# Turning x of the feed-forward: transposes of TensorE, or a DRAM write, a block read and 32x32 transposes of VectorE

## The chip, the cores and the metric

The kernel runs on one core of one Trainium2 chip. The metric is the time of one execution on the device in microseconds, as the median of several runs. The engines are TensorE (PE, its weight loads PEld), VectorE (DVE), ScalarE (ACT), GpSimd (POOL) and SyncE (SP), which only issues DMA transfers here.

## The reference

One block of a transformer with adaptive layer norm: linear attention, then a gated feed-forward, over 8192 tokens of 512 features.

```python
x = L0_attn_x                                  # (1, 8192, 512) float32
mod = (_silu(L0_c) @ L0_wmod).reshape(L0_c.shape[0], 6, 1, -1)
sa, ca, ga, sb, cb, gb = (mod[:, 0], mod[:, 1], mod[:, 2], mod[:, 3], mod[:, 4], mod[:, 5])
...
h = _layernorm(x, axis=-1) * (1 + ca) + sa
x = x + ga * _L0_attn_ref(h, ...)              # causal linear attention, 16 heads of 32
h = _layernorm(x, axis=-1) * (1 + cb) + sb
x = x + gb * _L0_ffn_ref(h, L0_ffn_w_gate, L0_ffn_w_up, L0_ffn_w_down)
...
# _L0_ffn_ref, weights int32, wg = w_gate / 127 and so on
gate = jnp.einsum('bsd,hd->bsh', x, wg)        # 512 -> 1536
up = jnp.einsum('bsd,hd->bsh', x, wu)
h = jax.nn.silu(gate) * up
return jnp.einsum('bsh,dh->bsd', h, wd)        # 1536 -> 512
```

## The kernel before

The kernel has two stages. The attention runs over 16 groups of 512 tokens up to some 1000 us; the feed-forward over 8 groups G of 1024 tokens (FT = 8 tiles of 128) fills the rest. Nothing is scheduled by a planner: each engine has its list of instructions, written out by hand, and waits on semaphores. An engine never goes past a wait that is not met.

**The steps of the feed-forward.** For its gate and up products a group needs x normalized and turned (features on the partitions). The 1536 hidden features are 12 blocks q. The 2x2 product of each block is done with seven products, p1 to p7 (L1859, four matmuls of 128x512 each, since both operands of x are split in a high and a low part), that go into four PSUM banks: xs (two), sums (two). In a step q (tensor `step`) TensorE issues p1(q), p7(q-1), p2(q), p5(q), p4(q-1), p6(q), p3(q). ScalarE copies p1, p5 and p6 out (save_p1, save_p5, save_u2), VectorE adds them up (add_c11 L1695, add_c12 L1701, add_c22 L1706) and multiplies with the gate (times_gate2 L1720, times_gate1 L1712), ScalarE and GpSimd split the product h in h_hi (L1586) and h_lo (h_low, L1488). In VectorE's step q the order is add_c22(q-1), add_c11(q), times_gate2(q-1), times_gate1(q-1), an aside, add_c12(q). Each product waits for the sum that frees its bank: p4(q) for add_c22(q), p5(q+1) for add_c12(q), p6(q) for add_c11(q).

**The halves.** After six blocks TensorE does the down products of that half (`down`, L1916, 8 row tiles into the banks dn[0..3]). p7(5) and p4(5) stand between the first ones: down 0, p7(5), down 1, p4(5), and so on. VectorE gates each result (gate_y, L1727) and GpSimd adds the residual (L1493), which SP has loaded (load_residual, L1402) and stores again. Before the last down the first three products of the next half or group are issued.

**The x of the next group.** SP loads it (load_x) into eight tiles xg: four of the attention's xg, two each of z_exp and z_relu. In the asides VectorE takes the statistics (norm_stats L1672, steps 2 to 5; norm_var in step 5), GpSimd makes rstd (rstd_of, L1483, behind h_low of q = 5), VectorE normalizes a pair of tiles at a time (norm_x, L1688, after add_c12(6) and in steps 7 to 9). TensorE turns: eight turns of four transposes (`turn`, L1927), 0 to 3 after steps 8 to 11 into dn, 4 to 7 between the downs into sums and xs. ScalarE evacuates each with scale and bias (evacuate, L1553) and makes the high parts (high, L1538). VectorE makes the four differences T1 to T4 (sum_of, L1662) and the low parts (low, L1666), in one long list behind step 11, with the gates of the second half between. The x of group 0 is turned by TensorE in the attention (x_turn L1088, turn_second L1096).

**The ring.** SP loads the weight parts of block q + 4 (load_parts, L1384, 1 MB) when p4(q) has freed their slot; stores, residuals, x and parts all stand in SP's one list.

## Time and profile before

| | |
|---|---|
| median of 3 runs | 2004.0 us (2003.52 to 2006.8) |
| the profiled execution | 2003.83 us, span 2002.1 us |
| TensorE busy | 1959.0 us, 98% |
| VectorE busy | 1455.2 us, 73% |
| ScalarE, GpSimd busy | 905.7 us, 869.1 us |
| moved by DMA | 309.81 MB |

The profile is one execution. Each engine's busy time is the sum of its instructions; a TensorE that is busy may still hold products that wait inside its pipeline, so stops are looked for in the timeline. The trace gives the start and duration of each instruction, and for an idle stretch before it the instruction that ended it.

### The profile page before, as it was taken

The numbers are of one execution on the slowest core, as the hardware profiler recorded it, in microseconds if no ns is written. First come the engines' busy times: TensorE is split into PE (matmuls) and PEld (weight loads), VectorE is DVE, ScalarE is ACT, GpSimd is POOL, SyncE is SP. The second block draws the span as 40 slices with busy tenths as digits, with TensorE's granted clock in tenths as the row PEclk, the third lists the DMA queues.
The fourth block names the chain that finished last, engine by engine and source line by source line (L and its number), as shares of the span: only waits on it lengthen the run. The fifth ranks groups of instructions, "written<-read, shape, count | busy, mean of one in ns | idle before, by whom it ended". The sixth has DMA issues, their size and how long they took to land. (4 is left out here: it accounts for less than half of the span.)

```text
span 2002.1 us, 43921 instructions
## 1 busy us (share of the span) xinstructions
PE 1959.0 (98%) x16008; PEld 1591.0 (79%) x16008; DVE 1455.2 (73%) x2409; ACT 905.7 (45%) x1542; POOL 869.1 (43%) x718
## 2 busy tenths in 40 slices
PE   7999999999999999999899999999999999999999
PEld 4788888888888888887678888888888888888887
DVE  7977888888888888887875857658576585765744
ACT  5443444344444344444254536445364453644533
POOL 2533544444544444443334444444434444344444
PEclk9999999999999999999999999999999999999999
DMA  7223333444433434433475654756546565465553
GB/s 268 70 90 104 117 118 119 130 134 127 127 112 121 135 121 136 129 101 99 152 284 178 209 172 148 228 168 210 174 147 224 168 210 182 143 219 170 170 170 106
DMA packets 202521, 309.81 MB, mean 155 GB/s; under 512 B 16145, under 2 KB 72977, under 8 KB 202386
## 3 DMA queue, kind: packets, MB, share of 16 engines
q1 hardware_dynamic: 201858, 306.78, 48.1%
q8 instruction: 107, 1.75, 0.4%
q10 hardware_dynamic: 528, 1.05, 0.1%
q14 instruction: 28, 0.23, 0.0%
HBM read 225.19 MB, written 82.58 MB: 154 GB/s over the span
## 5 line engine op out<-in xcount | busy, mean ns | idle before, releaser
L1488 POOL TENSOR_TENSOR h_lo<-y_rows,h_hi 128x512 fp32r<-128x512 f32 x192 | 246.5, 1303 | 368.1 <-ACT h_hi L1586 368.0
L460 POOL TENSOR_TENSOR x_res<-y,x_res 128x512 f32<-128x512 f32 x64 | 82.8, 1293 | 297.7 <-DVE y L871 287.8
L850 DVE TENSOR_TENSOR probs<-sc,causal 128x512 f32<-128x512 f32 x256 | 158.4, 679 | 5.4 <-PE sc L1147 5.2
L611 ACT ACTIVATE z_exp<-pj,qk_neg 128x512 f32<-128x512 f32 x128 | 87.9, 687 | 160.7 <-PE pj L1128 150.5
L1128 PE MATMUL pj<-xt_hi,w_hi 128*128 128x512 f32 x512 | 145.3, 405 | 12.0 <-DVE a_t L860 11.6
L1916 PE MATMUL sc<-wd,h_hi 128*128 128x512 f32 x384 | 150.6, 392 | 0.0
L1916 PE MATMUL sc<-wd,h_lo 128*128 128x512 f32 x384 | 149.7, 390 | 0.0
L449 POOL TENSOR_TENSOR a_lo<-a_t,a_hi 128x512 fp32r<-128x512 f32 x60 | 77.8, 1296 | 158.7 <-ACT a_hi L625 158.7
L1128 PE MATMUL pj<-xt_lo,w_hi 128*128 128x512 f32 x512 | 137.7, 390 | 1.7 <-DVE xt_lo L788 1.7
L1701 DVE TENSOR_TENSOR r_den<-pj,k_tok 128x512 f32<-128x512 f32 x96 | 66.2, 690 | 98.9 <-ACT k_tok L1569 54.6
L1128 PE MATMUL pj<-xt_hi,w_lo 128*128 128x512 f32 x512 | 137.3, 390 | 0.0
L1586 ACT ACTIVATE h_hi<-y_rows 128x512 fp32r<-128x512 f32 x192 | 119.0, 620 | 24.9 <-DVE y_rows L1720 13.4
L1564 ACT ACTIVATE k_tok<-sc 128x512 f32<-128x512 f32 x96 | 56.3, 586 | 158.7 <-PE sc L1859 158.7
L1128 PEld LDWEIGHTS pj<-xt_hi,w_hi 128*128 128x128 f32 x512 | 91.3, 188 | 39.2 <-DVE a_t L860 18.0
L596 ACT ACTIVATE xf<-sc,mod_col 128x512 f32<-128x512 f32 x64 | 49.9, 779 | 157.1 <-PE sc L1088 157.1
L444 POOL TENSOR_TENSOR prod<-k_sum,qt 128x512 f32<-128x512 f32 x64 | 94.4, 1475 | 61.1 <-DVE qt L796 42.2
L1128 PEld LDWEIGHTS pj<-xt_lo,w_hi 128*128 128x128 f32 x512 | 96.1, 188 | 23.1 <-DVE xt_lo L788 2.1
L1559 ACT ACTIVATE kv_diag<-pj 128x512 f32<-128x512 f32 x96 | 57.4, 598 | 123.3 <-PE pj L1859 122.5
L1128 PEld LDWEIGHTS pj<-xt_hi,w_lo 128*128 128x128 f32 x512 | 96.1, 188 | 20.5
L1574 ACT ACTIVATE k_sum<-r_den 128x512 f32<-128x512 f32 x96 | 60.7, 632 | 107.0 <-DVE y_rows L1712 94.4
L1712 DVE TENSOR_TENSOR y_rows<-sc,k_sum 128x512 f32<-128x512 f32 x96 | 66.3, 690 | 55.8 <-PE sc L1859 55.8
L1706 DVE TENSOR_TENSOR bv_row<-sc,kv_diag 128x512 f32<-128x512 f32 x96 | 66.3, 690 | 54.5 <-PE sc L1859 54.4
(247 smaller groups left out, 5403.5 us busy)
## 6 DMA issues: line engine op xcount, KB each, us to landing
w_hi<-parts SPq DMA_DIRECT2D x48, 1024.0 KB, 5.4
w_lo<-parts SPq DMA_DIRECT2D x48, 1024.0 KB, 5.3
x_mid<-x_res SPq DMA_DIRECT2D x96, 256.0 KB, 2.9
x_res<-in_L_attn_x SPq DMA_DIRECT2D x64, 256.0 KB, 2.8
k_dram<-k_block SPq DMA_DIRECT2D x252, 64.0 KB
xg<-in_L_attn_x SPq DMA_DIRECT2D x15, 1024.0 KB, 7.4
x_res<-x_mid SPq DMA_DIRECT2D x60, 256.0 KB, 4.0
full<-x_mid SPq DMA_DIRECT2D x60, 256.0 KB, 3.7
```

The costliest lines, as they stand in the source:

```text
L444: pool.tensor_tensor(out=prod[:, c % 2, :], in0=k_sum[:, c % 2, :], in1=qt[parity][:, c, :], op=ALU.mult).then_inc(prod_ready, 1)
L449: pool.tensor_tensor(out=a_lo[:, :], in0=a_t[:, :], in1=a_hi[:, :].bitcast(F32), op=ALU.subtract).then_inc(a_lo_ready, 1)
L460: pool.tensor_tensor(out=x_res[:, slot, :], in0=y[:, :], in1=x_res[:, slot, :], op=ALU.add).then_inc(y_ready, 1)
L611: act.activation(z_exp[:, n % 2, :], pj[:, n % 2, :], ACT.Relu, bias=qk_neg[:, 1 - kind, c:c + 1], scale=-scale).then_inc(below_ready, 1)
L850: dve.tensor_tensor(out=probs[:, h, :].rearrange("p (c i) -> p c i", c=C), in0=sc[:, h, :].rearrange("p (c i) -> p c i", c=C), in1=causal[ ...
L1128: mm = pe.matmul(to, w[:, k, at:at + P], xt[:, k, :], start=(i == 0), stop=(i == len(passes) - 1))
L1488: pool.tensor_tensor(out=h_lo[b], in0=h[i], in1=h_hi[b].bitcast(F32), op=ALU.subtract).then_inc(h_lo_ready, 1)
L1586: act.activation(h_hi[q % 6 * 2 + i], h[i], ACT.Copy).then_inc(h_hi_ready, 1)
L1701: dve.tensor_tensor(out=c12, in0=sums[1], in1=s12, op=ALU.add).then_inc(c12_ready, 1)
L1706: dve.tensor_tensor(out=c22, in0=xs[q % 2], in1=s5, op=ALU.add).then_inc(c22_ready, 1)
L1712: dve.tensor_tensor(out=h[0], in0=xs[q % 2], in1=gate[0], op=ALU.mult).then_inc(h1_ready, 1)
L1916: mm = pe.matmul(dn[i % 4], as_(part[j * 2 + t // GT][:, rows]), as_(wd[half * 6 + j]), start=(j == 0 and part is h_hi), stop=(j == 5 and ...
```

## The change

TensorE no longer turns x for groups 1 to 7. VectorE normalizes x as before; then SP writes each half of four tiles to a DRAM buffer xn_dram (save_xn, 1 MB) and reads it back in blocks (load_blocks: four transfers of 256 KB in runs of 512 bytes, each onto 32 partitions), so that 32 partitions hold the 32 tokens of a block for one quarter of the features. A 32x32 transpose of VectorE per bank (`turn`, 128x512, reading every fourth word) then writes the turned x to the same PSUM banks. The feature order that results is every fourth feature; the rows of the gate and up weights and of two modulation matrices are regrouped to it in their layout in DRAM, and TensorE's transposes for group 0 read every fourth word too. z_exp and z_relu become one buffer z.

The asides change: statistics in steps 1 to 4, norm_var in step 4, two pairs of norm_x in step 5 and two after add_c12(6) (group 0 keeps its statistics and norm_var, with two pairs after add_c12(6) and two in step 7). GpSimd makes rstd behind h_low of q = 4 (group 0: of q = 5). Turns 0 to 2 are asides of steps 9 to 11, turns 3 to 7 stand in the list behind step 11.

```diff
+        def regrouped(t, c):
+
+            return xg[:, t, :].rearrange("p (f c) -> p c f", c=C)[:, c, :]
+
         def x_turn(g, c, bank):
             wait(pe, xn_ready, g + 1)
             wait(pe, xf_ready, g * C + c - (C if isinstance(g, int) and g < 2 else 0))
             for t in range(GT):
-                mm = pe.transpose(bank[:, t * P:(t + 1) * P], xg[:, t, c * P:(c + 1) * P], ident[:, :])
+                mm = pe.transpose(bank[:, t * P:(t + 1) * P], regrouped(t, c) if isinstance(g, int) and g == NG
+                                  else xg[:, t, c * P:(c + 1) * P], ident[:, :])
             mm.then_inc(xt_ps, 1)
...
             for t in range(GT):
-                mm = pe.transpose(bank[:, t * P:(t + 1) * P], xg[:, t, c * P:(c + 1) * P], ident[:, :])
+                mm = pe.transpose(bank[:, t * P:(t + 1) * P], regrouped(t, c), ident[:, :])
             mm.then_inc(xt_ps, 1)
...
+        def save_xn(G, second):
+
+            wait(sp, xn_ready, G * 4 + (2 * second - 2))
+            sp.dma_start(xn_dram[second * GN:(second + 1) * GN, :].rearrange("(t p) d -> p t d", p=P),
+                         xg_halves[second][:, :, :]).then_inc(xn_out[second], 16)
+
+        def load_blocks(G, second):
+
+            wait(sp, xn_out[second], G * 16)
+            for h in range(HPC):
+                sp.dma_start(xg_halves[second][h * E:(h + 1) * E, :, :].rearrange("p t (b x) -> p (t b) x", x=P),
+                             xn_dram[second * GN:(second + 1) * GN, h * P:(h + 1) * P].rearrange("(b i) x -> i b x", i=E)
+                             ).then_inc(xb_in[second], 16)
...
+                    first = isinstance(G, int) and G == 0
+                    if not last and q == (6 if first else 5):
+                        save_xn(G + 1, 0)
                     if not last or q + 4 < HB:
                         load_parts(G, q + 4)
+                    if not last and q == (7 if first else 6):
+                        save_xn(G + 1, 1)
+                    if not last and first and q == 7:
+                        load_blocks(G + 1, 0)
+                    if not last and q == (8 if first else 7):
+                        load_blocks(G + 1, 1)
...
                     store(G, i)
+                    if i == 1 and not last and not (isinstance(G, int) and G == 0):
+                        load_blocks(G + 1, 0)
                     if not last or i + 3 < FT:
                         load_residual(G, i + 3)
...
                 if q not in (5, 11):
                     h_low(G, q, 1)
                     h_low(G, q, 0)
+                if q == 4 and ahead and not (isinstance(G, int) and G == 0):
+                    rstd_of(G + 1)
                 if q == 5:
                     h_low(G, q, 1)
                     h_low(G, q, 0)
-                    if ahead:
+                    if ahead and isinstance(G, int) and G == 0:
                         rstd_of(G + 1)
                     for i in range(FT):
                         residual(G, i)
...
+        def turn(G, i, bank):
+
+            k, which = divmod(i, 4)
+            c, second = (k, k + 2, k, k + 2)[which], which // 2
+            wait(dve, xb_in[second], G * (16 * HPC))
+            if i >= 4:
+                wait(dve, (c11_ready, c12_ready, h1_ready, h1_ready)[which], G * HB + (0, 0, -1, 0)[which])
+            wait(dve, y_gated, G * 16 + (FT - 2 * FT))
+            dve.transpose(bank.rearrange("p (b i) -> p b i", i=E),
+                          xg_halves[second][:, :, :].rearrange("p t (b e c) -> p c (t b) e", c=C, e=E)[:, c, :, :]
+                          ).then_inc(xt_ps, 1)
...
-                if ahead and not first and 2 <= q < 6:
-                    norm_stats(G + 1, q - 2)
-                if ahead and q == 5:
+                if ahead and not first and 1 <= q < 5:
+                    norm_stats(G + 1, q - 1)
+                if ahead and q == (5 if first else 4):
                     norm_var(G + 1)
-                if ahead and 7 <= q < 10:
-                    norm_x(G + 1, q - 6)
+                if ahead and not first and q == 5:
+                    norm_x(G + 1, 0)
+                    norm_x(G + 1, 1)
+                if ahead and first and q == 7:
+                    norm_x(G + 1, 2)
+                    norm_x(G + 1, 3)
+                if ahead and q >= 9:
+                    turn(G + 1, q - 9, dn[q - 9])
...
             if ahead:
-                norm_x(G + 1, 0)
+                for pair in range(2) if isinstance(G, int) and G == 0 else range(2, 4):
+                    norm_x(G + 1, pair)
...
+            turn(G + 1, 3, dn[3])
             sum_of(G + 1, T1, 0)
+            turn(G + 1, 4, sums[0])
             sum_of(G + 1, T2, 0)
             add_c22(G, 11)
+            turn(G + 1, 5, sums[1])
             sum_of(G + 1, T3, 0)
             times_gate2(G, 11)
             low(G + 1, T1, 0)
             times_gate1(G, 11)
+            turn(G + 1, 6, xs[0])
+            turn(G + 1, 7, xs[1])
             sum_of(G + 1, T4, 0)
             for op in (T2, B22, T3, B11, B21, T4):
                 low(G + 1, op, 0)
...
-        def turn(G, i, bank):
-
-            k, which = divmod(i, 4)
-            c, second = (k, k + 2, k, k + 2)[which], which // 2
-            wait(pe, xn_ready, G * 4 + (2 * second - 2))
-            for t in range(GT):
-                mm = pe.transpose(bank[:, t * P:(t + 1) * P], xg[second * GT + t][:, c * P:(c + 1) * P], ident[:, :])
-            mm.then_inc(xt_ps, 1)
...
                 for q in range(first + 1, first + 6):
                     step(G, q)
-                    if ahead and q >= 8:
-                        wait(pe, y_gated, G * 16 + FT)
-                        turn(G + 1, q - 8, dn[q - 8])
...
                 down(G, i + 1, range(4))
                 p4(G, first + 5)
                 if half and ahead:
-                    wait(pe, c11_ready, G * HB + HB)
-                    turn(G + 1, 4, sums[0])
-                    wait(pe, c12_ready, G * HB + HB)
-                    turn(G + 1, 5, sums[1])
-                    wait(pe, h1_ready, G * HB + (HB - 1))
-                    turn(G + 1, 6, xs[0])
                     wait(pe, xf_ready, G * 8 + 4)
                 down(G, i + 2, range(4))
-                if half and ahead:
-                    wait(pe, h1_ready, G * HB + HB)
-                    turn(G + 1, 7, xs[1])
                 down(G, i + 3, range(4))
...
+REGROUPED = np.arange(D).reshape(P, C).T.reshape(D)
+
+
 def word_blocks(w_gate, w_up, w_down):
-    w_gate, w_up = (np.asarray(w).reshape(HB, P, C, P).transpose(0, 2, 3, 1) for w in (w_gate, w_up))
+    w_gate, w_up = (np.asarray(w)[:, REGROUPED].reshape(HB, P, C, P).transpose(0, 2, 3, 1) for w in (w_gate, w_up))
...
         if name == "L0_wmod":
-            layouts.append(("in_wmod_t", a.T))
+            turned = np.ascontiguousarray(a.T).reshape(6, D, D)
+            for m in (SB_MOD, CB_MOD):
+                turned[m] = turned[m, REGROUPED]
+            layouts.append(("in_wmod_t", turned.reshape(6 * D, D)))
```

## Rows read from the trace of the kernel before

**Rows 1.** The page, part 1: busy us, share of the span, instructions.

```profile
PE 1959.0 (98%) x16008; PEld 1591.0 (79%) x16008; DVE 1455.2 (73%) x2409; ACT 905.7 (45%) x1542; POOL 869.1 (43%) x718
```

**Rows 2.** The line of the turn, one bank: durations, first and last start.

```profile
L1927 PE MATMUL sc<-ident,xg x28: 270/272/273, 1089.7 to 1837.8; 128*128 128x128 f32 x28
```

**Rows 3.** Timeline, TensorE: start us, us, line, out<-in, count [idle before, releaser].

```profile
1154.35 0.73 PE L1859 MATMUL sc<-w_lo,w_hi 128*128 128x512 f32 x2
...
1160.88 0.73 PE L1859 MATMUL sc<-w_lo,w_hi 128*128 128x512 f32 x2
...
1207.44 0.60 PE L1927 MATMUL num<-ident,xg 128*128 128x128 f32 x4
...
1214.28 0.60 PE L1927 MATMUL sc<-ident,xg 128*128 128x128 f32 x4
```

**Rows 4.** Timeline, TensorE, end of a group: turn 3, and p6 of the next.

```profile
1227.96 0.38 PE L1927 MATMUL state<-ident,z_exp 128*128 128x128 f32 x2
...
1256.74 0.68 PE L1859 MATMUL sc<-w_lo,w_hi 128*128 128x512 f32 x2
```

**Rows 5.** Timeline, VectorE, same stretch: add_c12, sum T1, sum T4, low T2, add_c11.

```profile
1228.94 0.69 DVE L1701 TENSOR_TENSOR r_den<-pj,k_tok 128x512 f32<-128x512 f32 x1 [1.82 <-ACT k_tok L1569]
1230.07 1.47 DVE L1662 TENSOR_TENSOR full<-xf 128x512 f32<-128x512 f32 x1 [0.44 <-ACT xf L1553]
...
1235.19 1.47 DVE L1662 TENSOR_TENSOR full<-r_den,full 128x512 f32<-128x512 f32 x1
1236.58 1.77 DVE L1666 TENSOR_TENSOR xt_hi<-full,w_lo 128x512 fp32r<-128x512 f32 x1
...
1255.89 0.67 DVE L1695 TENSOR_TENSOR r_den<-pj,k_tok 128x512 f32<-128x512 f32 x1
```

**Rows 6.** Timeline, GpSimd, same stretch: the pair of h_low beside sum T1.

```profile
1228.45 2.54 POOL L1488 TENSOR_TENSOR h_lo<-y_rows,h_hi 128x512 fp32r<-128x512 f32 x2 [4.29 <-ACT h_hi L1586]
```

**Rows 7.** The line of the attention's block transpose: ns min/median/max, first and last start.

```profile
L844 DVE STREAM_TRANSPOSE k_block<-kt x63: 659/669/712, 63.0 to 978.6; 128x512 f32<-128x512 f32 x63
```

**Rows 8.** Groups by line: busy us, mean ns | idle before and releasers.

```profile
L803 DVE TENSOR_TENSOR_SCAN k_sum<-kt,k_past 128x512 f32<-128x512 f32 x60 | 80.2, 1337 | 5.1 <-DVE kt L796 2.3
...
L1088 PEld LDWEIGHTS sc<-ident,xg 128*128 128x128 f32 x272 | 33.4, 140 | 10.4 <-DVE xg L774 1.9 <-issue 0.5
```

**Rows 9.** Timeline, VectorE: last statistics in step 5; a pair of norm_x.

```profile
1165.54 1.28 DVE L1672 BATCH_NORM_STATS2 stats<-z_relu 128x6 f32<-128x512 f32 x2
...
1199.99 0.99 DVE L1688 TENSOR_SCALAR xg<-xg,mean_var,rstd 128x512 f32<-128x512 f32 x2
```

**Rows 10.** Timeline, GpSimd: the pair of h_low of q = 4; rstd.

```profile
1166.95 2.54 POOL L1488 TENSOR_TENSOR h_lo<-y_rows,h_hi 128x512 fp32r<-128x512 f32 x2 [3.98 <-ACT h_hi L1586]
...
1174.87 1.65 POOL L1483 TENSOR_TENSOR rstd<-var_eps,half_neg 128x8 f32<-128x8 f32 x1
```

**Rows 11.** Timeline, TensorE: p4(5), and p6(6).

```profile
1170.99 0.61 PE L1859 MATMUL sc<-w_hi,w_lo 128*128 128x512 f32 x2
...
1192.75 0.61 PE L1859 MATMUL sc<-w_lo 128*128 128x512 f32 x2
```

**Rows 12.** Busy us in a stretch: PE, PEld, DVE, ACT, POOL, granted clock, DMA, GB/s.

```profile
984.00:985.00 1.00, 1.00 (x3) 0.74 (x3) 1.00 (x3) 0.00 (x0) 0.00 (x0) 0.50 0.60 100
```

**Rows 13.** Timeline, TensorE: products behind three waits at the attention's end.

```profile
974.34 1.19 PE L1197 MATMUL pj<-w_hi,a_hi 128*128 128x512 f32 x4 [2.00 <-DVE a_lo L781]
...
983.25 1.97 PE L1197 MATMUL pj<-w_hi,a_hi 128*128 128x512 f32 x4 [2.73 <-DVE a_lo L781]
...
986.72 1.15 PE L1197 MATMUL pj<-w_hi,a_lo 128*128 128x512 f32 x4
...
1002.02 0.73 PE L1859 MATMUL sc<-w_hi,w_lo 128*128 128x512 f32 x2 [2.44 <-DMA w_lo<-parts]
```

**Rows 14.** Timeline, GpSimd: a residual of the first half.

```profile
1186.54 1.29 POOL L1493 TENSOR_TENSOR x_res<-a_t,x_res 128x512 f32<-128x512 f32 x1 [1.11 <-DMA x_res<-x_mid]
```

**Rows 15.** The page, part 6: issues, KB each, us to landing.

```profile
w_hi<-parts SPq DMA_DIRECT2D x48, 1024.0 KB, 5.4
```

More of the change, by code:

```diff
@@ L43 @@
 Signals = namedtuple("Signals", "wide_ready wd_in xt_ps xf_ready a_ready y_gated y_ready y_out xr_ready state_ready op_ready pj_ready part_out b_ready sum_made b_high")
-Shared = namedtuple("Shared", "xg xf h_hi h_lo ring b_hi b_lo full wd silu_sum saved gate h y x_res gb_row pairs sums dn")
+Shared = namedtuple("Shared", "xg xg_halves xf h_hi h_lo ring b_hi b_lo full wd silu_sum saved gate h y x_res gb_row pairs sums dn")
 Turned = namedtuple("Turned", "kt qt v r_den probs prod k_block k_sum a_hi a_lo")
@@ L82, in build @@
         k_dram = nc.dram_tensor("k_dram", (P, D), F32, kind="Internal").ap()
+        xn_dram = nc.dram_tensor("xn_dram", (FT * P, D), F32, kind="Internal").ap()
         gb_dram = nc.dram_tensor("gb_dram", (1, D), F32, kind="Internal").ap()
@@ L143, in build @@
                                       x_mid, k_dram, parts, downs)
-        ffn = feed_forward(sem, later, ident, mod_col, half_neg, norm, gb_dram, parts, att, shared, x_mid, out)
+        ffn = feed_forward(sem, later, mod_col, half_neg, norm, gb_dram, parts, att, shared, x_mid, xn_dram, out)
         block = top.enter_context(nc.Block())
@@ L190, in attention @@
     xg, stats, mean_var, var_eps, rstd, x_in, ln_chain, var_ready, rstd_ready, xn_ready = norm
-    z_exp = sbuf(s, "z_exp", [P, 2, GN])
-    z_relu = sbuf(s, "z_relu", [P, 2, GN])
+    z = sbuf(s, "z", [P, 4, GN])
+    z_exp, z_relu = z[:, 0:2, :], z[:, 2:4, :]
     kt, qt, v, r_den, probs, prod, k_block, k_sum, a_hi, a_lo = turned
@@ L231, in attention @@
                                                                sem("exp_ready"), sem("phi_ready"))
-    v_ready, ksum_ready, prod_ready, prod_turned = sem("v_ready"), sem("ksum_ready"), sem("prod_ready"), sem("prod_turned")
+    v_ready, ksum_ready, prod_ready = sem("v_ready"), sem("ksum_ready"), sem("prod_ready")
     past_ready, gb_ready, gb_saved = sem("past_ready"), sem("gb_ready"), sem("gb_saved")
@@ L258, in attention @@
     flat_diag = kv_diag[:, :, :].rearrange("p c f -> p (c f)")
-    shared = Shared([xg[:, t, :] for t in range(GT)] + [z[:, i, :] for z in (z_exp, z_relu) for i in range(2)],
+    shared = Shared([xg[:, t, :] for t in range(GT)] + [z[:, i, :] for z in (z_exp, z_relu) for i in range(2)], [xg, z],
                     [xf[:, 0, :], xf[:, 1, :], r_den[0][:, 0, :], r_den[0][:, 1, :]],
@@ L1312, in attention, with feed_forward @@
     return Programs(sync, gpsimd, scalar, vector, tensor), signals, shared
-def feed_forward(sem, later, ident, mod_col, half_neg, norm, gb_dram, parts, att, shared, x_mid, out):
+def feed_forward(sem, later, mod_col, half_neg, norm, gb_dram, parts, att, shared, x_mid, xn_dram, out):
     stats, mean_var, var_eps, rstd = norm[1:5]
-    xg, xf, h_hi, h_lo, (blocks, filled), b_hi, b_lo, full, wd, total, saved, gate, h, y, x_res, gb_row, xs, sums, dn = shared
+    xg, xg_halves, xf, h_hi, h_lo, (blocks, filled), b_hi, b_lo, full, wd, total, saved, gate, h, y, x_res, gb_row, xs, sums, dn = shared
     c11, c12, c22 = total
@@ L1327, in feed_forward @@
     xt_ps, xf_ready = sem("fxt_ps"), sem("fxf_ready")
+    xn_out, xb_in = [sem(f"xn_out{i}") for i in range(2)], [sem(f"xb_in{i}") for i in range(2)]
     gb_in, gb_chain, gb_done = sem("gb_in"), sem("gb_chain"), sem("gb_done")
```

## The prediction

> **What bounds the kernel now.** I read the page first: TensorE is busy for 98% of the span [rows 1]. A busy share can hide short waits, so I then went to the timeline of TensorE in the feed-forward. It is nearly gapless there: a step without a turn lasts 1160.88 - 1154.35 = 6.53 us, one with a turn at its end 1214.28 - 1207.44 = 6.84 us [rows 3], and a group (1837.8 - 1089.7) / 6 = 124.7 us [rows 2]. So TensorE sets the time, and what is taken from it counts, if no other engine comes late. The two places where one can are where the change puts its work: the end of a group, and step 5 of the first half.
>
> At the end of a group, from the last product of step 11 (turn 3 follows it at 1227.96) to p6 of the next group (1256.74), TensorE needs 28.78 us [rows 4]. VectorE's list for that stretch starts with add_c12 at 1228.94 and ends with add_c11 at 1255.89, whose 0.67 us end 0.2 us before p6, which waits for it [rows 5]. In between VectorE has one idle gap of 0.44 us. So VectorE is here as late as TensorE: the slack is about 0.2 us. Part of its time is lost to GpSimd: a VectorE instruction with two SBUF inputs that meets a GpSimd one ends 0.55 us after that has ended (sum T1: 1230.07 + 1.47 = 1231.54, GpSimd's pair ends at 1228.45 + 2.54 = 1230.99) [rows 5, 6].
>
> **What is removed.** 8 turns x 7 groups on TensorE (224 transposes). Turns 0 to 2 lie in steps 9 to 11: each saves 6.84 - 6.53 = 0.31 us [rows 3], 0.9 us a group. Turns 3 to 7 lie in the stretch of 28.78 us. It holds 116 products (92 of seven downs with p7 and p4, 12 of p1, p2, p5, 12 of the last down); at a step's 6.53 us for 28 they are 27.1 us, so the five turns are 1.7 us. That part only counts if VectorE keeps up there.
>
> **What VectorE gets: 8 transposes a group.** No row shows one that writes PSUM or reads at a step of four words. The nearest is the block transpose of the attention, 128x512, 0.669 us (0.659 to 0.712) [rows 7]; back to back such instructions start some 0.60 us apart. The far end of the bound is the slowest one-input pass over 512 columns in the trace, the scan, 1.34 us [rows 8]. I take 0.67, the row of the same operation. Turns 0 to 2 stand ahead of add_c12, in a slot where VectorE sat idle 1.82 us [rows 5]: free, at either bound, since the blocks should have landed long before. Turns 3 to 7 lie in the full stretch. Turn 3 falls into the idle gap and into the wait of sum T1 for GpSimd, whose end it leaves where it is: free. Turns 4 to 7 push the rest: 4 x 0.60 = 2.4 us. Turns 6 and 7 stand ahead of sum T4 and low T2, which now lose 0.8 and 1.1 us to the two h_low of GpSimd (1.47 and 1.77 instead of 0.68) [rows 5]; with the turns between, the first h_low passes beside them and only one wait is left: -0.9. So add_c11 and p6 come 1.5 us later, and TensorE's own 1.7 us are swallowed. Bounds: 0.6 (no push but one) and 4 (1.34 us each).
>
> The Trainium skill (SBUF — State Buffer, SBUF: two separate sides) says that SBUF is read in 16-byte lines and that accesses that change the line each time pay a penalty. The turn reads every fourth word, a new line each time; by this rule, whose penalty the page does not size, it would take up to twice 0.67 us at an estimate, and the sum would be 2042 instead of 2035, the first half of rival 1; no row here shows it.
>
> **What is moved: the norm of the next x.** In groups 1 to 6, norm_x of the first four tiles goes into step 5, ahead of add_c12(5) and add_c22(5) on VectorE. It waits for rstd, and GpSimd makes rstd behind h_low of q = 4. That pair runs 1166.95 to 1169.49, and rstd takes 1.65 us [rows 10]: ready at 1171.15. VectorE's slot begins at 1165.54 [rows 9], so it stands still for 5.6 us. Two norm pairs (0.99 us each [rows 9], 1.9 in all), add_c12 (0.6) and add_c22 (0.7) follow: 1174.4. p4(5) waits for add_c22(5) and starts now at 1170.99 [rows 11], straight behind its predecessor. So TensorE stands still for about **3.5 us** in each of 6 groups. What follows p4(5) (down, gates, residuals) is shifted as a whole and gives nothing back, since TensorE had no slack there. Bounds: 3.2 and 3.8, as far as the rows repeat. The other moves I take at nothing. Statistics one step earlier are 1.28 us [rows 9] in a slot with 1.82 us of idle [rows 5]; norm_var goes from behind the last statistics of step 5 to the same place of step 4; behind add_c12(6) stand two norm pairs for one, 0.99 us more, ahead of an add_c22(6) that p4(6) wants two products later. What hides them is that slot ahead of add_c12 and its like; without it each costs what it is over, under 1 us.
>
> **The clock.** A stop of TensorE can cost more than itself. At the end of the attention it waited 2.73 us up to 983.25. The granted clock behind that is 0.50, 1.2 of 2.4 GHz [rows 12]: eight products take 986.72 - 983.25 = 3.47 us. Behind a wait of 2.00 us, at 974.34, four take 1.19, and eight then some 2.0: 1.5 us were lost. Behind 2.44 us, at 1002.02, two take 0.73 us, the full rate [rows 13]. A stop of 3.5 us is longer than all three, but it stands between dense products, unlike that one. I take a fall in half of the six stops: 3 x 1.5 = 4.6 us; bounds 0 and 9.2.
>
> **Transfers.** 2 MB more written and 2 MB read in a group, on SP's queue. save_xn(0) waits on SP, ahead of load_parts(9), which waits for p4(5) anyway. load_blocks(0) goes between store(1) and load_residual(4): four issues and 1 MB are put ahead of a residual that GpSimd already waits for at 1186.54 [rows 14]. From there the residual (1.3), a gate and add_c11(6) (0.7 each) take until 1189.2, and p6(6) wants that at 1192.75 [rows 11]: 3.5 us of slack. A transfer of 1 MB takes 5.4 us to landing [rows 15]; if the residual stands behind the whole of it, it is up to 2 us too late. The nearest row has the residual landing with SP's other transfers in flight, so I take nothing; bound 0 to 2 us a group. In group 0 all is one to two steps later: load_blocks(0) is issued only behind load_parts(11), and turn 0 may wait for three megabytes: 1 us taken, 0 to 3, once. The strided reads of the 32 transposes in the attention: at most 32 x 0.14 us, a second weight load [rows 8], 4.5; I take 0.5, since weight loads run beside products. The regrouped weight rows change no instruction.
>
> **The sum.** The profiled execution took 2003.83 us (span 2002.1), the median of the runs is 2004.0: 0.2 apart, within their spread. A group 1 to 6: +3.5 (p4(5)) + 1.5 (end) - 0.9 (turns 0 to 2) = +4.1, x 6 = 24.6. Group 0: 1.5 - 0.9 + 1.0 = 1.6. Clock 4.6, attention 0.5. Total 31.3: 2003.8 + 31.3 = **2035**. Its own range by the bounds: 2022 (no fall of the clock, 0.6 at the end) to 2045.
>
> **Rivals.**
> 1. Slower still: the turn at a step of four words takes 1.2 us or more, and the blocks queue ahead of the residual. Three of the four pushes of 0.55 us stay, less what more of GpSimd's time they cover: +1.0 x 7 = 7; a residual 2 us over its slack, x 6 = 12. 2042 to 2054, **2050** with both halves. For: nothing in the trace reads so, and GpSimd already waits for that DMA. Against: 0.67 us in all 63 rows of the nearest form; 3.5 us of slack. It decides from a turn of 1.0 us or a residual 3.5 us late.
> 2. Even: VectorE takes the turns in stride at the end of the group (GpSimd's waits cover all of them), so that 0.9 + 1.7 = 2.6 us a group come off TensorE, x 7 = 18.2, and the stop at p4(5), x 6 = 21, eats it: **2006**. For: 1.9 us of VectorE's stretch are waits. Against: two thirds of it are pure work, and four turns are 2.4 us.
> 3. Faster, on the other side: as 2, and rstd is in time, since GpSimd reaches it before VectorE does; then all of 18.2 us stay: **1986**. It decides from the order of h_low(4) and the norm: were h_low(4) over by 1164, there would be no stop. Against: h_low(4) follows ScalarE's h_high(4), which stands in step 5 itself.
> That the turns stay on TensorE is excluded by the text of the change.
>
> **How the numbers follow.** Forecast 0.62, rival 1 0.22, rival 2 0.08, rival 3 0.08. The range leaves out rivals 2 and 3 and takes in rival 1 and the low bound: 2017 to 2055. About 0.2% (4 us) can be told from no change. Faster: rival 3 and a little of rival 2, 0.09; within: 0.07 (rival 2 without the rest); slower 0.84.
>
> **What would show it.** In the profile after: GpSimd's rstd (8 columns) right behind the pair of q = 4, VectorE idle some 5.6 us before the first norm of each group 1 to 6, and TensorE idle some 3.5 us before p4(5) six times; a granted clock under 1 behind some of them; the turn near 0.67 us; TensorE idle at p5, down 7 and p6 of the next group, 1.5 us later from turn 3's old place than before; steps 9 to 11 of 6.53 us. The prediction is wrong if p4(5) shows no stop, or if a group is shorter than 124.7 us.

## The result

The changed kernel takes 2070.4 us (median of 4 runs, 2067.6 to 2071.6) against 2004.9 us for the kernel before on the same chip: a ratio of 1.0325 [1.0313, 1.0338]. The prediction said 2035 with a range of 2017 to 2055: right about the side, wrong about the size, and the time lies above the range. The profiled execution has a span of 2068.3 us.

The first line of the page, with [rows 1] as its counterpart, looks almost as before:

```profile
PE 1960.5 (95%) x15784; PEld 1577.8 (76%) x15784; DVE 1495.3 (72%) x2465; ACT 905.4 (44%) x1542; POOL 872.6 (42%) x718
```

TensorE has 224 instructions fewer, and its share fell from 98% to 95%: it stands still more. Where, the view of waits says, here of TensorE from 1020 us (the feed-forward) to the end: line, what it waited for, us in total, times, the longest. The kernel before has no wait worth a line there.

```profile
PE sc L1917 <- DVE bv_row L1752: 30.1, 19, 3.1
PE num L1974 <- DVE a_t L1773: 18.7, 7, 2.7
PE sc L1917 <- DVE r_den L1741: 9.2, 6, 1.8
PE pj L1917 <- DVE r_den L1747: 7.1, 1, 7.1
```

Of 65.6 us of waits, these 65.1 are TensorE waiting for VectorE; bv_row is written by add_c22, a_t by gate_y, r_den by add_c11 (L1741) and add_c12 (L1747; this one wait is group 0's). The timeline of TensorE in one group shows which products these are (start, us, engine, line, count, and in brackets the wait ahead):

```profile
1318.71 0.94 PE L1917 MATMUL sc<-w_hi,w_lo 128*128 128x512 f32 x2 [3.15 <-DVE bv_row L1752]
...
1344.17 0.73 PE L1917 MATMUL sc<-w_lo 128*128 128x512 f32 x2 [1.81 <-DVE r_den L1741]
...
1350.47 0.73 PE L1917 MATMUL sc<-w_hi,w_lo 128*128 128x512 f32 x2 [0.56 <-DVE bv_row L1752]
...
1385.31 0.73 PE L1917 MATMUL sc<-w_hi 128*128 128x512 f32 x2 [1.14 <-DVE bv_row L1752]
...
1396.45 0.50 PE L1974 MATMUL num<-wd,h_hi 128*128 128x512 f32 x1 [2.67 <-DVE a_t L1773]
```

In order: p4(5), p6(6), p4(6), p4(11), and down 12. From turn 0 of one group to that of the next it is (1900.44 - 1098.41) / 6 = 133.7 us, for 124.7 before [rows 2].

Three sums split the span of each kernel below: the stops of TensorE from 1020 us on (the view of waits), the time lost to the clock from there on (each stretch of 6 us times one minus its granted clock), and the rest. The rest holds the attention too, with its own falls of the clock: they cost 1.7 us before and 5.1 after, and 1.7 to 5.1 in the other runs.

| kernel | measured us | span | stops | clock | rest |
|---|---|---|---|---|---|
| before | 2004.9 | 2002.1 | 0.0 | 0.8 | 2001.3 |
| after | 2070.4 | 2068.3 | 65.6 | 16.2 | 1986.5 |
| e1 rstd early | 2047.3 | 2045.5 | 47.0 | 16.1 | 1982.4 |
| e2 blocks late | 2056.6 | 2052.9 | 52.6 | 19.1 | 1981.3 |
| e3 words in a row | 2064.5 | 2060.8 | 60.2 | 12.6 | 1988.0 |
| e4 all three | 2026.3 | 2024.5 | 26.9 | 14.2 | 1983.4 |
| e5 five edits | 2017.1 | 2017.5 | 23.3 | 11.4 | 1982.8 |
| e6 gate 8 early | 2077.5 | 2074.0 | 66.3 | 19.3 | 1988.4 |
| e7 norm alone | 2033.6 | 2032.2 | 19.1 | 11.1 | 2002.0 |
| e8 five, end in order | 2012.0 | 2010.7 | 15.2 | 0.3 | 1995.2 |
| e9 end in order alone | 2069.0 | 2067.2 | 57.6 | 15.9 | 1993.7 |
| e10 = e8, add_c11 early | 2003.1 | 2000.2 | 8.8 | 0.1 | 1991.3 |
| e11 = e9, words in a row | 2063.4 | 2060.9 | 51.5 | 11.9 | 1997.5 |
| e12 = e10, three moves | 2001.7 | 1999.5 | 9.3 | 0.0 | 1990.2 |

The change does take work off TensorE: the rest falls by 14.8 us, although it holds 3.4 us more of the attention's clock. It pays for that with 65.6 us of stops and 15.4 us of clock: -14.8 + 65.6 + 15.4 = +66.2, the difference of the spans.

### The profile page after: what moved, and what is told of

It is laid out like the page before. It is cut to its first block and busy times, and to the rows that moved or that the text cites. A ratio compares the mean times of both kernels' runs of the same rounds, so it can differ in the third digit from the quotient of the medians.

```text
span 2068.3 us, 43621 instructions
## 1 busy us (share of the span) xinstructions
PE 1960.5 (95%) x15784; PEld 1577.8 (76%) x15784; DVE 1495.3 (72%) x2465; ACT 905.4 (44%) x1542; POOL 872.6 (42%) x718
## 5 line engine op out<-in xcount | busy, mean ns | idle before, releaser
L612 ACT ACTIVATE z<-pj,qk_neg 128x512 f32<-128x512 f32 x128 | 87.8, 686 | 162.4 <-PE pj L1134 159.9
L1747 DVE TENSOR_TENSOR r_den<-pj,k_tok 128x512 f32<-128x512 f32 x96 | 66.2, 690 | 87.6 <-ACT k_tok L1603 43.2
L1525 POOL TENSOR_TENSOR x_res<-a_t,x_res 128x512 f32<-128x512 f32 x30 | 45.1, 1504 | 125.8 <-DVE a_t L1773 85.1
L1758 DVE TENSOR_TENSOR y_rows<-sc,k_sum 128x512 f32<-128x512 f32 x96 | 66.2, 689 | 43.3 <-PE sc L1917 43.1
```

The lines of the kernel that those rows point to most:

```text
L612: act.activation(z_exp[:, n % 2, :], pj[:, n % 2, :], ACT.Relu, bias=qk_neg[:, 1 - kind, c:c + 1], scale=-scale).then_inc(below_ready, 1)
L1747: dve.tensor_tensor(out=c12, in0=sums[1], in1=s12, op=ALU.add).then_inc(c12_ready, 1)
L1758: dve.tensor_tensor(out=h[0], in0=xs[q % 2], in1=gate[0], op=ALU.mult).then_inc(h1_ready, 1)
```

## The experiments

**Do the stops add up?** The question is whether each stop has a cause of its own, so that the gains add up, or whether a stop that is taken away comes back at the next place. Three edits take one cause each, and a fourth run has all three.

GpSimd makes rstd ahead of the two h_low of step 4, not behind them:

```diff
+ if q == 4 and ahead and not (isinstance(G, int) and G == 0): rstd_of(G + 1)
  if q not in (5, 11): h_low(G, q, 1); h_low(G, q, 0)
- if q == 4 and ahead and not (isinstance(G, int) and G == 0): rstd_of(G + 1)
```

> The changed kernel with GpSimd's rstd put ahead of the h_low pair of q = 4 (groups 1 to 6), nothing else. Theory A (the stops of TensorE stand one behind the other and add up): the stop ahead of p4(5), 3.14 us in 6 groups, is gone, and with it the falls of the clock that follow it (about half of eight falls, 1.7 us each): 2070 - 19 - 7 = 2044, at least 2051 if the clock then falls at the next stop instead. Theory B (what is late there is made late by something else, and TensorE waits for it at the next place, p6(6)): the stop moves, 2065 to 2070.

Measured: 2047.3 us (ratio 1.0209 [1.0192, 1.0226]), 23 less than after. In the changed kernel the timelines of GpSimd and VectorE show the wait that this takes away; h_low(4) and rstd above, norm_x, add_c12 and add_c22 below:

```profile
1446.48 2.54 POOL L1520 TENSOR_TENSOR h_lo<-y_rows,h_hi 128x512 fp32r<-128x512 f32 x2 [3.98 <-ACT h_hi L1620]
1448.97 1.65 POOL L1515 TENSOR_TENSOR rstd<-var_eps,half_neg 128x8 f32<-128x8 f32 x1
...
1450.66 1.91 DVE L1722 TENSOR_SCALAR xg<-xg,mean_var,rstd 128x512 f32<-128x512 f32 x4 [5.50 <-POOL rstd L1515]
1452.49 0.68 DVE L1747 TENSOR_TENSOR r_den<-pj,k_tok 128x512 f32<-128x512 f32 x1
1453.09 0.68 DVE L1752 TENSOR_TENSOR bv_row<-sc,kv_diag 128x512 f32<-128x512 f32 x1
```

VectorE stands still 5.50 us, does two norm pairs and two adds, and TensorE's p4(5) begins at 1453.82, 3.14 us late. With the edit the stop at p4(5) is gone (18.9 us in six groups), and p6(6) waits 2.2 us more in all. The clock loses as much as before, since it now falls behind other stops.

The first half's block reads go behind the residual loads, into step 6:

```diff
- if i == 1 and not last and not (isinstance(G, int) and G == 0): load_blocks(G + 1, 0)
- if not last and first and q == 7: load_blocks(G + 1, 0)
+ if not last and q == (7 if first else 6): load_blocks(G + 1, 0)
```

> The changed kernel with the block read of the first half moved on SP's list from between store(1) and load_residual(4) to behind load_parts(10), in groups 1 to 6. Theory A: the residual of tile 4, which lands 7.3 us after its issue behind 1 MB of blocks, lands in 4 us as before; the stop of 1.5 to 1.8 us at p6(6) and part of the 0.55 us at p4(6) go, 6 times: 2070 - 10 to -13 = 2057 to 2060. Theory B (the queue is slow for the whole of that stretch, whoever stands in it): the residual stays late, 2068 to 2070.

Measured: 2056.6 us (1.0260 [1.0243, 1.0277]), 14 less. In the changed kernel SP issues the four block reads, then the load of residual 4, and GpSimd gets that residual 7.28 us after its issue (1467.51 to 1474.79):

```profile
1465.06 2.18 SPq L1415 DMA_DIRECT2D xg<-xn_dram  x4
1467.51 0.99 SPq L1423 DMA_DIRECT2D x_res<-x_mid  x1
...
1474.79 1.28 POOL L1525 TENSOR_TENSOR x_res<-a_t,x_res 128x512 f32<-128x512 f32 x1 [6.51 <-DMA x_res<-x_mid]
```

Before it was 3.9 us (issued at 1182.61, used at 1186.54 [rows 14]), and with the edit it is 4.0 (1197.44 to 1201.42); the issue before, then issue and use in e2:

```profile
1182.61 0.34 SPq L1402 DMA_DIRECT2D x_res<-x_mid  x1
```

```profile
1197.44 0.35 SPq L1423 DMA_DIRECT2D x_res<-x_mid  x1
...
1201.42 1.29 POOL L1523 TENSOR_TENSOR x_res<-a_t,x_res 128x512 f32<-128x512 f32 x1 [1.13 <-DMA x_res<-x_mid]
```

Behind the residual stand gate 6, add_c11(6) and p6(6); the stops at p6(6) and p4(6) are gone.

The turn reads 32 words in a row, where it read every fourth word; the weight rows are regrouped to match, and group 0 is turned on TensorE by 16 products of 32 columns a bank:

```diff
- xg_halves[second][:, :, :].rearrange("p t (b e c) -> p c (t b) e", c=C, e=E)[:, c, :, :]
+ xg_halves[second][:, :, :].rearrange("p t (b c e) -> p c (t b) e", c=C, e=E)[:, c, :, :]
- REGROUPED = np.arange(D).reshape(P, C).T.reshape(D)
+ REGROUPED = np.arange(D).reshape(HPC, C, E).transpose(1, 0, 2).reshape(D)
```

> The changed kernel with another regrouping of the features, so that VectorE's turn reads 32 words in a row instead of every fourth; for group 0 TensorE turns with 16 small products per bank in place of 4 transposes (up to +5 us in all). Theory A (the step of four words makes the turn 1.09 us): the turn falls to 0.67 to 0.70 us, and at the end of a group p4(11) and down 12 are up to 4 x 0.4 = 1.6 us less late, 7 times: 2070 - 11 = 2059, less where falls of the clock go as well. Theory B (writing PSUM makes it so): the turn stays at 1.09 us, 2070 to 2075.

Measured: 2064.5 us (1.0301 [1.0284, 1.0318]), 6 less, where theory A expected 11. The line of the turn (ns min/median/max), first in the changed kernel, then here:

```profile
L1733 DVE STREAM_TRANSPOSE sc<-z x21: 1049/1104/1133, 1111.1 to 1924.6; 128x512 f32<-128x512 f32 x21
```

```profile
L1738 DVE STREAM_TRANSPOSE sc<-z x21: 676/706/718, 1110.8 to 1916.9; 128x512 f32<-128x512 f32 x21
```

So writing PSUM costs next to nothing (0.71 us for the 0.67 of [rows 7]); the step of four words costs 0.40 us. The stops fall by 5.4 us and the clock by 3.6, but the rest rises by 1.5, and the small products are the likely reason: up to the first product of the feed-forward, without stops and clock, TensorE needs 957 to 959 us in the seven runs that have them and 953 to 956 in the other seven. Some 3.5 us of what the shorter turn gives are lost there.

> All three edits together: rstd early, block read late, turn of words in a row. Theory A, that the stops add up: the three gains sum, 26 + 11 + 11 = 48 us, about 2022, with the 7 us stop of group 0 and some stop at the end of each group left. Theory B, that they stand beside each other and the longest decides: not more than the largest alone, about 2045.

Measured: 2026.3 us (1.0104 [1.0087, 1.0120]), 44 less; the three gains sum up to 23 + 14 + 6 = 43. Theory A holds for these stops. What was left is down 12's wait for gate 8 (15.7 us) and about one fall of the clock in each group.

**Is the norm's move alone enough for its stop?** The kernel before, with the statistics, rstd and norm_x moved as in the change, and nothing else:

```diff
- if ahead and not first and 2 <= q < 6: norm_stats(G + 1, q - 2)
+ if ahead and not first and 1 <= q < 5: norm_stats(G + 1, q - 1)
+ if ahead and not first and q == 5: norm_x(G + 1, 0); norm_x(G + 1, 1)
```

> The kernel before, with one part of the change alone: statistics one step earlier, the reciprocal roots behind the lows of step 4, normalising in step 5 and behind add_c12 of step 6. TensorE still turns x; no write to DRAM, no block reads, no turns on VectorE. Theory A (the stop at p4 of unit 5 comes from this order alone): 6 stops of 3.14 us and up to one clock fall of 1.7 us behind each, 2005 + 19 to 29 = 2024 to 2034. Rival B (the stop needs the turns and the transfers too, by a VectorE that is later as a whole): under 1 us in a group, 2004 to 2011.

Measured: 2033.6 us (1.0149 [1.0132, 1.0166]), +29.8, the upper end of theory A. The waits of TensorE in the feed-forward are the six stops and hardly more:

```profile
PE sc L1866 <- DVE bv_row L1708: 18.9, 6, 3.1
```

The clock cost 11.1 - 0.8 = 10.3 us, that is six falls of 1.7 us, one with each stop. No transfer and no turn is needed for either.

**What ends a group?** First the gate of down 8 was put four places up in VectorE's list, since down 12 waits for it:

```diff
- for op in (T2, B22, T3, B11, B21, T4): low(G + 1, op, 0)
- sum_of(G + 1, T1, 1)
+ for op in (T2, B22, T3): low(G + 1, op, 0)
  gate_y(G, FT)
+ for op in (B11, B21, T4): low(G + 1, op, 0)
+ sum_of(G + 1, T1, 1)
```

> The changed kernel with one edit: VectorE gates down unit 8 four operations earlier (ahead of three lows and a sum), so that TensorE's down unit 12 has its bank. Theory A (the stop of 2.67 us ahead of down 12, seen in all seven groups, is a cost of its own; VectorE then has up to 2 us of slack at the next group's p6): the stop falls to under 0.5 us, 1 to 2 us of it come back at the head of the next group, and two to four clock falls of 1.7 us go: 2052 to 2062. Rival B (VectorE's list already ends the group): the stop moves to p6 of unit 0 in full, 2068 to 2072. Rival C (nothing comes back): 18.7 us and all falls behind it, 2040 to 2047.

Measured: 2077.5 us (1.0371 [1.0354, 1.0389]), 7 more than after, outside all three expectations. TensorE, then VectorE, then GpSimd:

```profile
1394.05 0.50 PE L1976 MATMUL num<-wd,h_hi 128*128 128x512 f32 x1 [0.29 <-DVE a_t L1773]
1399.49 0.50 PE L1976 MATMUL sc<-wd,h_hi 128*128 128x512 f32 x1 [2.43 <-DVE y L1773]
...
1393.92 0.68 DVE L1700 TENSOR_TENSOR xt_hi<-xf,w_hi 128x512 fp32r<-128x512 f32 x1
1394.52 1.78 DVE L1700 TENSOR_TENSOR xt_hi<-r_den,w_hi 128x512 fp32r<-128x512 f32 x1
...
1394.15 1.60 POOL L1525 TENSOR_TENSOR x_res<-a_t,x_res 128x512 f32<-128x512 f32 x1 [3.12 <-DVE a_t L1773]
```

Down 12's stop is down to 0.29, and down 13 stops for 2.43 in its place, for gate 9. The early gate lets GpSimd start its residual early, and that meets the low of B21, which takes 1.78 us for 0.68. The expectation looked for the stop at p6 and missed the next unit of the same loop. By the table the stops are as long as after (66.3 us for 65.6); the longer time is 3.1 us of clock, two falls more, and 1.9 of rest.

Then this edit together with the three of e4 and, in group 0, the block reads ahead of load_parts(11).

> The three edits of the run before it together (the reciprocal roots ahead of the lows of step 4, the block reads behind the residuals, the turn reading 32 words in a row), and two more: the gate of down unit 8 four places earlier in VectorE's list, and in group 0 the block reads of the first half ahead of the partial sums' load. Theory A (each stop is paid on its own; 2026.3 with three edits, where 15.7 us of stops at down 12 and 5.3 at group 0's first turn were left): the gate takes away about 2 us in each of 7 groups, of which a part comes back as a wait at the head of the next group, 1 to 2 us net, 7 to 14 in all, and some clock falls of 1.7 us; group 0 gives back 5 and a fall of about 3. 2003 to 2012. Rival B (VectorE's list, longer by eight turns, is by now what ends a group, so that a gate done earlier only moves the wait to the next group's p6): 2018 to 2024.

Measured: 2017.1 us (1.0067 [1.0051, 1.0084]): above the 2003 to 2012 of theory A, below the 2018 to 2024 of rival B, with the same 17.0 us of stops at down 13. What it gained against e4 came from group 0, whose first turn now waits 1.1 us for its blocks, for 7.9 in e4 and 9.3 in the changed kernel; its turn 2, for the second half, waits 3.0 us there, and TensorE 1.8 behind it.

So the whole order was changed: gates 8, 9 and 10 close to the moment their downs are done, and add_c22(11) ahead of turn 4; once alone and once with the five edits.

```diff
+ add_c22(G, 11)
  turn(G + 1, 4, sums[0]); sum_of(G + 1, T2, 0)
- add_c22(G, 11)
  ...
+ gate_y(G, FT); low(G + 1, B11, 0); low(G + 1, B21, 0)
+ gate_y(G, FT + 1); low(G + 1, T4, 0); sum_of(G + 1, T1, 1); gate_y(G, FT + 2)
```

> The changed kernel with the order of VectorE's list at the end of a group alone put right: gates of down 8, 9, 10 earlier, add_c22 of unit 11 ahead of turn 4. The other stops stay. Theory A (the two stops at the end of a group, 2.67 and 1.14 us in 7 groups, come from the order of the list; some 3.8 us of slack ahead of the next p6 is there in the changed kernel): 3.8 x 7 = 26.7 us go and some falls of the clock, 1 to 2 us a group come back at p6: 2070 - 14 to 27 = 2043 to 2056. Rival B (eight turns of 1.10 us make VectorE's list the bound): 2062 to 2072.

Measured: 2069.0 us (1.0326 [1.0311, 1.0340]): no difference from after; rival B. TensorE at the end of the group, then VectorE's gate 13 and add_c11 of the next:

```profile
1390.70 0.50 PE L1977 MATMUL num<-wd,h_hi 128*128 128x512 f32 x1 [0.57 <-POOL h_lo L1520]
1393.66 0.50 PE L1977 MATMUL num<-wd,h_hi 128*128 128x512 f32 x1 [0.85 <-DVE a_t L1773]
1402.98 0.73 PE L1920 MATMUL sc<-w_hi 128*128 128x512 f32 x2 [0.50 <-DVE xt_hi L1700]
1409.82 0.72 PE L1920 MATMUL sc<-w_lo,w_hi 128*128 128x512 f32 x2 [0.81 <-DVE r_den L1741]
...
1408.40 0.69 DVE L1773 TENSOR_TENSOR y<-sc,ga_row 128x512 f32<-128x512 f32 x1 [0.66 <-POOL full L1525]
1409.00 0.68 DVE L1741 TENSOR_TENSOR r_den<-pj,k_tok 128x512 f32<-128x512 f32 x1
```

Two stops of together 3.81 us became four of together 2.73, and add_c11, the end of VectorE's list, stands where it stood (28.31 us behind the start of turn 3, at 1409.00; 28.05 and 1409.11 in the changed kernel). The stops fall by 8.0 us, and the rest rises by 7.2. The clock is lost as before, 15.9 us: the falls behind down 12 went to p4(5) of the next group.

> The five edits of the run before it, with VectorE's list at the end of a group put in another order: the gates of down 8, 9 and 10 stand three or fewer operations apart from the moment that their down units are done, and add_c22 of unit 11 stands ahead of turn 4. Nothing is added or taken away. Theory A (what is left of the loss are stops behind the wrong order of one list: 17.0 us ahead of down 13 and 6.6 ahead of p4, and a clock fall behind the former; VectorE's list ends 2 us or more ahead of the next group's p6): both stops fall under 0.5 us a group, 5 to 10 us of clock go with them, up to 1 us a group comes back at p6 of unit 0: 1982 to 1996, below the kernel before. Rival B (VectorE's list as a whole is the bound at the end of a group): the stops come back at the next group's p6, 2008 to 2018. Rival C (GpSimd's residuals now start within the lows and stretch them by 1.1 us each): the gain is halved, 1998 to 2006.

Measured: 2012.0 us (1.0036 [1.0024, 1.0048]). Rival B's number, but not its mechanism alone: the long stops are gone and so are the falls of the clock (16.2 us in the changed kernel, 11.4 in e5, 0.3 here). Against e5 stops and clock give 19.2 us, but the rest takes 12.4 of them back. Four short stops remain in each group, the longest of 0.80 us at p6 for add_c11. Whether this one comes from add_c11's place behind gate 13 or from the length of the list, the next pair tells: one run with add_c11 one gate earlier, ahead of gates 13 to 15 (the expectation counts three) and the product with gate 2 of unit 11 ahead of turn 5, one with the end in order and shorter turns.

```diff
  gate_y(G, FT + 4)
- gate_y(G, FT + 5)
  add_c11(G + 1, 0)
+ gate_y(G, FT + 5)
```

> The best version so far (2012.0) with two more moves in VectorE's list at the end of a group: add_c11 of the next group's unit 0 three gates earlier than its place (behind the gate of down 12, ahead of those of 13 to 15), and the product with gate 2 of unit 11 ahead of turn 5. Theory A (what is left is the place of add_c11: p6 of unit 0 waits 0.80 us a group for it, and down 8 0.34 us for the lows of unit 11): 7 x 0.8 to 1.1 go: 2004 to 2007. Rival (the stop at p6 of unit 0 comes from the lows, not from add_c11): 2010 to 2013.

Measured: 2003.1 us (0.9992 [0.9983, 1.0001]): 9 less, the stop at p6 gone (two moves were made at once; the stop at down 8 stayed). In e9 and e8 the gate ahead of add_c11 waited 0.66 us for a residual of GpSimd, with which it shares a buffer of y; that wait stood in the chain.

> The run of the end of the group alone (2069.0) with the turn reading 32 words in a row (0.70 us for 1.10), nothing else. Theory A (with the order put right, the length of VectorE's list from turn 3 on sets the end of a group, so a shorter turn counts in full there): five turns x 0.40 = 2.0 us in each of 7 groups, less 1.4 us more for the smaller products at the end of the attention, and up to 2 us of group 0's stop: 2069 - 12 to 16 = 2053 to 2057. Rival (the list's length is not the bound; a shorter turn gives what it gave alone, 6 us): 2062 to 2066.

Measured: 2063.4 us (1.0295 [1.0281, 1.0309]): 5.6 less than e9, the rival's number, what the shorter turn gave in e3 too. The rest is 3.8 us above e9's, as the small products in the attention would make it. The list from turn 3 to add_c11 takes 1406.99 - 1379.51 = 27.48 us here and 1409.00 - 1380.69 = 28.31 in e9: only 0.83 shorter, where five turns save 2.0. The low of T2, in both kernels the first behind sum T4, shows where it went; here, then in e9:

```profile
1388.03 1.77 DVE L1705 TENSOR_TENSOR xt_hi<-full,w_lo 128x512 fp32r<-128x512 f32 x1
```

```profile
1391.12 0.68 DVE L1700 TENSOR_TENSOR xt_hi<-full,w_lo 128x512 fp32r<-128x512 f32 x1
```

With shorter turns VectorE is there while GpSimd still works on the lows of unit 11, and loses 1.1 us to it: 2.0 - 1.1 = 0.9. The prediction counted 0.9 for the same effect, turns that keep VectorE out of GpSimd's way. In the changed kernel it was more, as sum T4 and low T2 show, which take 1.5 us less than the 1.47 and 1.77 of [rows 5]:

```profile
1390.56 1.02 DVE L1696 TENSOR_TENSOR full<-r_den,full 128x512 f32<-128x512 f32 x1
1391.50 0.68 DVE L1700 TENSOR_TENSOR xt_hi<-full,w_lo 128x512 fp32r<-128x512 f32 x1
```

The shorter turns give 1.1 us of it back.

Last, three more moves on top of e10: ScalarE's and VectorE's part of unit 11 earlier, gates 8 and 9 one place up, and the low of T4 back.

> The version before it (2003.05) with three more moves at the end of a group: unit 11's two products with their gates, and ScalarE's high parts of them, ahead of the third sum (down 8 waits 0.47 us a group for their lows); the gates of down 8 and 9 one place earlier (down 12 waits 0.25); the low of T4 behind those of B11 and B21 of the second half (the next group's p1 waits 0.50). Theory A (each of the three stops goes, with the pipeline's restart behind it, some 0.2 us each): 7 x 1.2 to 1.8 = 8 to 13 us: 1990 to 1995, faster than the kernel before (2005.4). Rival (GpSimd's residuals, started earlier, meet one more of VectorE's operations on SBUF and stretch it by 1.1 us, and the list's end is late again): 1998 to 2004.

Measured: 2001.7 us (0.9994 [0.9985, 1.0003]): not told apart from e10 or from the kernel before, and within the rival's range. Of the three stops only that of down 8 is gone, and one of the same size stands at down 15, for gate 11 (3.8 us in 7 groups); down 12 and the next group's p1 wait as long as in e10.

## Why the prediction was wrong

The forecast and the trace by the same terms, in us over the whole run:

| term | forecast | measured |
|---|---|---|
| TensorE's own work, with the attention | -6.3 - 11.9 + 0.5 = -17.7 | -14.8 (rest) |
| stop at p4(5) | 6 x 3.5 = 21 | 18.9 |
| end of a group | 7 x (1.5 + 1.7) = 22.4 | 7 x (2.67 + 1.14) = 26.7 |
| residual behind the blocks | 0 | 9.2 + 3.3 = 12.5 |
| group 0's first turn | 1.0 | 7.1 |
| clock | 4.6 | 15.4 |

The sums are 31.3 and 65.8; two stops of 0.5 us in all make up the 66.2.

The forecast missed by 35 us. Of these 18.6 are the transfers (residual and group 0), which it put at 1.0, and 10.8 the clock. Its range was narrower than its own bounds, too: the upper ones (3.8 at p4(5), 4 at the end of a group, 9.2 of clock, 2 a group for the residual, 3 in group 0, 4.5 in the attention) add up to 42 us over 2035, and it stopped at 2055.

**Right.** The stop at p4(5): VectorE's wait of 5.6 us was measured as 5.50, the stop of 3.5 as 3.14, and e1 and e7 show it by taking it away and by making it alone. Steps 9 to 11 last 6.54 us, as forecast. The other moves of statistics and norms cost nothing: the 0.55 at p4(6), behind the four tiles of norm_x, goes with the late residual (it is gone in e2 and not there in e7).

**Transfers: the step that failed most.** "The nearest row has the residual landing with SP's other transfers in flight, so I take nothing; bound 0 to 2 us a group." The row [rows 14] was of loads of 256 KB among their like. Behind 1 MB in four issues the load took 7.3 us for 3.9, and it was issued 2.90 us behind the store ahead of it, for 0.95; the slack of 3.5 us was read right and used up. The upper bound, 2 us x 6, was what happened (12.5 with p4(6)), and e2 takes it away. Group 0 is the same step: 1 us taken, 3 bounded, and VectorE waited 9.28 (TensorE 7.1), which e5 takes away by putting the block reads ahead of load_parts(11):

```profile
1098.41 1.09 DVE L1733 STREAM_TRANSPOSE num<-xg 128x512 f32<-128x512 f32 x1 [9.28 <-DMA xg<-xn_dram]
```

**The clock.** Half of six falls of 1.5 us were taken. That a stop brings a fall was right, the count was too low: there are seven falls in the groups, of some 1.7 us, and a longer one behind group 0's stop (3.4 us). [Rows 12, 13] show a fall behind a wait of 2.73 us and none behind 2.00 and 2.44; taking one in two from that was a guess. In e7 all six stops of 3.15 us brought one. In the changed kernel five of the six stops at p4(5) and two of the seven at down 12 did, this one of 2.67 us among them; columns as in [rows 12]:

```profile
1398.00:1400.00 2.00, 2.00 (x7) 1.52 (x6) 2.00 (x3) 1.33 (x3) 2.00 (x2) 0.50 0.18 66
```

Eight products stand 0.43 us apart for 0.23. The falls don't go with the number of stops. With two long stops a group the clock loses 16.2 us, with either of them taken away 16.1 (e1, where some fall behind p6(6)'s stops of 1.5 to 2.3 us) and 15.9 (e9), and with both and the others gone 0.1 (e10). In the ten runs whose groups hold a stop of 1.8 us or more there are five to nine falls in the groups, about one a group; so one was to be counted for every group with such a stop. What decides which stop brings a fall isn't shown.

**The end of a group** came near in size (26.7 for 22.4) by luck, through errors that cancel. The turn takes 1.10 us, not 0.67: the far end of the bound, 1.34, was nearer than the row of the same operation. The prediction weighed the rule of the Trainium skill (SBUF — State Buffer, SBUF: two separate sides) that an access which changes the line pays a penalty. The trace agrees in kind, with 1.10 against 0.71 us, not the twice that was estimated. The 2042 given for that twice doesn't follow from the prediction's own bound of 4 us a group at 1.34 us, which makes 2035 + 7 x 2.5 = 2052. And the stops stand elsewhere. The prediction followed the end of VectorE's list to p6 of the next group; it didn't follow gate 8, which stands behind five turns in that list and for which down 12 waits (gate 8 at 1395.72, down 12 at 1396.45), nor add_c22(11), behind turn 4, for p4(11) (at 1385.31):

```profile
1384.59 0.66 DVE L1752 TENSOR_TENSOR bv_row<-sc,kv_diag 128x512 f32<-128x512 f32 x1
...
1395.72 0.68 DVE L1773 TENSOR_TENSOR a_t<-num,ga_row 128x512 f32<-128x512 f32 x1
```

P6 itself then doesn't wait: TensorE is late already. The list behind a moved instruction was named in the prediction, but not each of its readers.

**Rival 1** (slower still, 2050) was the nearest: both signs that it named came true, the turn over 1.0 us and the residual late. It had no more clock in it than the forecast and no more of group 0, and these are what it lacked.

**Rival 3**, that the turns come off TensorE for nothing, is what e10 and e12 came to by order and the shorter turn, and they gain nothing that can be measured. Their rest is 10 to 11 us below the kernel before, and about 9 us of short stops give it back; some 3.5 us of the rest are group 0's small products in the attention.

**Open.** The rest isn't constant: it is 1981 to 1988 where the long stops stand and 1990 to 1998 in the kernels with the reordered end (e8 to e12). One part is that a stop costs more than the view of waits lists. In e10:

```profile
1363.48 0.39 PE L1981 MATMUL state<-wd,h_lo 128*128 128x512 f32 x1
1364.34 0.50 PE L1981 MATMUL num<-wd,h_hi 128*128 128x512 f32 x1 [0.47 <-POOL h_lo L1525]
1364.68 0.40 PE L1981 MATMUL num<-wd,h_lo 128*128 128x512 f32 x1
```

Without a stop two products start 0.23 us apart. Here it is 0.86, of which 0.47 are listed (the view counts from the end of the product ahead, 0.39 behind its start), and then 0.34: a stop costs 0.16 + 0.11 = 0.27 us on top. With 34 stops in e8 for 14 in e5 that is 5.4 of the 12.4 us by which e8's rest is longer; where the others come from stays open.

## What to carry to other kernels

When an engine gets work in the middle of its list, follow every later entry of the list to its readers, not only the last one: here the gate of a down unit and an add stood behind the turns, and putting one of them right moved the stop to the next. A load that is issued behind a large one on the same queue comes late (by 3.4 us behind 1 MB here); large prefetches belong behind the small loads that somebody waits for. Count about one fall of the clock for each group of work that holds a long stop, however many it holds, and don't expect it back before the last of them is gone. And add up the upper bounds before a range is given.

## What the runs showed of the hardware

- VectorE's 32x32 block transpose of 128x512 words into PSUM takes 0.71 us when it reads 32 words in a row, and 1.10 when it reads every fourth.
- Stops of 1.8 to 3.15 us between dense products were followed by a granted clock of 0.50 in some cases and not in others: all six stops of 3.15 us in e7, two of seven of 2.67 us in the changed kernel, six of seven of some 2.4 us in e5, two of 1.8 and 1.9 us in e1. At that level eight products take 3.4 us for 1.8.
- A stop costs TensorE 0.27 us more than its listed wait (0.86 and 0.34 us from start to start for 0.23 each, with 0.47 listed, in e10).
- A load of 256 KB issued behind four block reads of 256 KB each was used 7.3 us after its issue, and 3.9 us without them.
- One VectorE instruction with two inputs in SBUF that meets one of GpSimd takes up to 1.78 us for 0.68; an earlier start of either moves the meeting to another instruction.
